# Self-attention's set-up reordered: coarse maxima first, sent by halves, and maxima 8 couples ahead instead of 10

## The chip, the cores and the metric

The kernel runs on one core of one Trainium2 chip. The metric is the device time of one execution in microseconds (us), median over several runs. All times below are microseconds from the span's start unless they say otherwise.

## The reference, cut to what matters

The whole reference is a decoder of two layers (self-attention, cross-attention and a feed-forward part in each, with layer norms between them). The change touches only the first self-attention:

```python
NUM_HEADS = 16                                   # x is (2, 1024, 256), heads of 16
q = x @ Wq.T * (1.0 / jnp.sqrt(D)); k = x @ Wk.T; v = x @ Wv.T
scores = jnp.einsum('bqhd,bkhd->bhqk', q, k)     # 1024 x 1024 for each of 2 x 16 heads
attn = jax.nn.softmax(scores, axis=-1)
out = jnp.einsum('bhqk,bkhd->bqhd', attn, v).reshape(B, S, D)
return out @ Wff.T + bff
x = _layernorm(x + _L0_attn_ref(x, ...), axis=-1)
```

## The kernel before, in words

The kernel is a row of stages, one after the other, and `stage_a` is the first self-attention. A generator, `schedule()`, yields jobs in one order, and each engine's function walks the whole list and does its own part of each job. So the order of the list is the order of work on PE (`tensor`), DVE (`vector`), ACT (`scalar`), POOL (`gpsimd`) and SP (`sync`), and an engine that waits holds back all that stands behind it in its own list.

**Jobs of the set-up.** `xt` i transposes one 128-row tile of X on PE, and ACT copies it to XT. `prep` (b, gi, half, which) is a projection of 512 columns: two matmuls in f32 (four instructions) for Q (`which` 0) or K (`which` 1). ACT writes the coarse part (a_QH or a_KH, fp32r), and DVE writes the rest (a_QL or a_KL, the result less the coarse part). `stack` k sends twelve pieces of 128 KB from these into QS[k % 3] and KS[k % 3]: for each of two head groups e, three blocks of 16 rows. Q holds coarse, fine, coarse, and K holds coarse, coarse, fine, so that one matmul over 48 rows gives a product of nearly full precision. For k = 0, SP sends six and ACT sends six; a later k goes by SP alone, for k of 2 and more as single `part` jobs spread over units. `edges` (DVE: 11 operations, then four transposes on PE) and `parts` (DVE: copies and small operations on their result) prepare a scatter into a matrix `adj` in DRAM, which a later stage reads; `prep_v` projects V.

**Jobs of the steady part.** There are 16 units u (batch, group of four heads, half of the queries). Unit u has 16 couples `s` (u, j): two matmuls of scores, and one DVE reduction over 128x1024 that gives row maxima (a_MX, line 741). `row` u folds them (a_MM), `m` u transposes the result, ACT copies it to a_MT, and SP sends it to DRAM (a_m), waits for that landing and sends it back as row 48 of QS, twice. Then come the unit's 16 slots n with two jobs `st` each: a matmul over 64 rows that gives the scores less the maximum, transposed, and ACT's exponential to a_P (line 847). `pv` multiplies by V. In slot n the schedule also yields a couple `s` of a unit ahead: ten couples ahead of `st` in the kernel before, with `row` u + 1 in slot 5 and `m` u + 1 in slot 8. `spread` (slot 3), `recip` (slot 7) and `scale` handle the softmax sums of unit u - 1 through DRAM (a_s, a_SQ, a_RQ, a_r, a_RB), on SP's queue as well. The `part` jobs stand in slots 4 to 15 of units 1, 2, 4, 6, 8 and 10, and a `prep` may overwrite the coarse and fine parts only after the pieces read from them have landed (`stacked`).

The list `between` puts jobs between the couples `s` that are done ahead of the first `st`. PE takes the banks 0 to 3 in pairs for `s` and `prep` of k = 0, and the banks 4 to 6 in turn for `st`, `xt`, `prep_v` and others.

Of the kernel before, what the change touches and what calls it, by code (L numbers as in the profile page):

```python
# [8 lines left out]
F32 = mybir.dt.float32  # L9
# [397 lines left out]
def stage_a(K, block):  # L407
# [33 lines left out]
    stack_in = [K.landing() for _ in range(3)]  # L441
    m_out = [K.landing() for _ in range(2)]
# [14 lines left out]
    U = [(b, g4, qh) for b in range(2) for g4 in range(4) for qh in range(2)]  # L457

    def schedule():
        for i in range(8):  # L460
            yield "xt", i
        for half in range(2):
            for which in range(2):
                yield "prep", 0, 0, half, which
        yield "powers",
        yield "stack", 0
        yield "edges",
        for kt in range(3):
            yield "prep_v", 0, kt
        yield "parts",  # L470
        between = {10: [("stack", 1)], 12: [("ctx", 0), ("ctx", 1)]}
        for kt in range(3, 8):
            between.setdefault(kt - 2, []).append(("prep_v", 0, kt))
# [4 lines left out]
        for i in range(6):  # L478
            between.setdefault(14 + 2 * i, []).append(("zero", i))
# [28 lines left out]
        for j in range(10):  # L508
            yield "s", 1, j
            yield from between.get(16 + j, ())  # L510
        for u in range(16):
            for n in range(16):
                yield "st", u, n, 0
                if n < 6 and u + 1 < 16:
                    yield "s", u + 1, n + 10
                if n >= 6 and u + 2 < 16:
                    yield "s", u + 2, n - 6
                if n == 5 and u + 1 < 16:
                    yield "row", u + 1
                yield "st", u, n, 1  # L520
                if n == 8 and u + 1 < 16:
                    yield "m", u + 1
                if n == 1 and u:
                    yield "pv", u - 1, 7
                    yield "turn_ou", u - 1
                if n > 1 and n % 2:
                    yield "pv", u, n // 2 - 1
                yield from late.get((u, n), ())
                if u:
                    if n == 3:  # L530
                        yield "spread", u - 1
                    if n == 7:
                        yield "recip", u - 1
                    if n == 11:
                        yield "scale", u - 1
                if n % 4 == 2 and step < E.LOTS:
                    yield "edge", step
                    step += 1
                if n % 8 == 0:
                    k = 2 * u + n // 8  # L540
                    yield "sums", k
                    if k % 8 == 7:
                        yield "lot", k // 8
                if n in (1, 6, 11):
                    yield "send", u, n
# [35 lines left out]
    def stacked(b, gi):  # L581

        k = 4 * b + 2 * gi
        return [(stack_in[i % 3], 12 * (i // 3 + 1)) for i in (k - 2, k - 1) if i >= 0]

    def tensor(_):
        free = {}

        def bank_free(bk):
            if bk in free:  # L590
                pe.wait_ge(*free[bk])

        for job in jobs:
# [44 lines left out]
            elif kind == "s":  # L638
# [5 lines left out]
                pe.wait_ge(stack_in[k % 3], 12 * (k // 3 + 1))  # L644
                bank_free(bk)
                for e in range(2):
                    rows = slice(64 * e, 64 * e + 48)
                    ins = mm(pe, bank(bk + e), QS[k % 3][rows, cc, qh * 512 + qt * 128:qh * 512 + qt * 128 + 128],
                             KS[k % 3][rows, cc, 512 * kh:512 * kh + 512])
# [8 lines left out]
            elif kind == "st":  # L658
# [4 lines left out]
                pe.wait_ge(m_in[u % 2], 2 * (u // 2 + 1))  # L663
                bank_free(bk)
# [43 lines left out]
    def vector(_):  # L708
        for i in range(2):
            v.e.memset(KS[i][:, :, :].bitcast(F32), 1.0)  # L710
            v.e.memset(QS[i][:, :, :].bitcast(F32), 0.0).then_inc(*fill[i].up())
# [7 lines left out]
        for job in jobs:  # L719
# [10 lines left out]
            elif kind == "edges":  # L730
# [65 lines left out]

    def scalar(_):
        s.wait_ge(eps_pool, 1)
        for job in jobs:
# [23 lines left out]
            elif kind == "powers":  # L823
                E.powers_act(s)
            elif kind == "stack" and a[0] == 0:
                for i in range(1, 12, 2):
                    stack(s, 0, i)
# [39 lines left out]
    def gpsimd(_):  # L867
# [6 lines left out]
        g.step(g.e.memset(KS[2][:, :, :].bitcast(F32), 1.0))  # L874
        g.step(g.e.memset(QS[2][:, :, :].bitcast(F32), 0.0), fill[2])
# [31 lines left out]
    def sync(_):  # L907
        def load_x(i):
            dma(sp, X[:, 4 * i:4 * i + 4, :],
                A["x"].rearrange("b (t p) d -> p (b t) d", p=128)[:, 4 * i:4 * i + 4, :]).then_inc(*x_in[i].up())  # L910

        def load(n, W, landed):
            dma(sp, W, A[n].rearrange("(c p) n -> p c n", p=128)).then_inc(*landed.up())

        load_x(0)
        load_x(1)
        load("L0_attn_WqT", WL[0], wq_in)
        load("L0_attn_WkT", WL[1], wk_in)
        load("L0_attn_WvT", WV[:, :, :], wv_in)
        load_x(2)  # L920
        load_x(3)
        E.edges_sp(sp)
        dma(sp, CX, A["ctx_1024"].rearrange("b s d -> s b d")).then_inc(*cx_in.up())
        for job in jobs:
            kind, *a = job
            if kind == "stack":
                for i in range(0, 12, 1 if a[0] else 2):
                    stack(sp, a[0], i)
            elif kind == "part":
                stack(sp, *a)  # L930
            elif kind == "weights":

                for k in (6, 7):
                    sp.wait_ge(stack_in[k % 3], 12 * (k // 3 + 1))
# [2654 lines left out]
```

## Time and profile before

| | |
|---|---|
| median of 3 runs | 2444.74 us (2443.32 to 2446.77) |
| span of the profiled execution | 2451.3 us (no other time is given with it) |
| PE, DVE, ACT, POOL busy | 93%, 62%, 45%, 43% of the span |
| first matmul | 4.92 us |
| first reduction of maxima | 34.44 us |
| first `st` of unit 0 | 70.08 us |
| first `st` of unit 15 | 473.16 us |

The profile is of one execution. It has a timeline for each engine, busy times by window with TensorE's granted clock (as a share of 2.4 GHz), waits by releaser, and the chain of work that ended last, which goes back from the last instruction to whatever released each step.

### The profile page before, as it was taken

To read this page: it belongs to the slowest core of one execution; us is meant where nothing else is said; L and a number is where in the kernel's file an instruction comes from. 1 tells how busy PE (TensorE), PEld (TensorE's weight loads), DVE (VectorE), ACT (ScalarE), POOL (GpSimd) and SP (SyncE) were. 2 spreads that over 40 slices of the span, in tenths; PEclk is the share of its full clock that TensorE was granted. 3 is DMA by queue.
4 is the path that set the end of the run, shared out by engine and by line. 5 is a ranking of instruction groups with operands and counts; after the bars stand their busy time and mean duration, and the time that the engine had idled before them with its cause. 6 is when DMAs were issued, how large, how long until landed. Compare 5 with 4: busy or idle time off the path is not lost.

```text
span 2451.3 us, 34108 instructions
## 1 busy us (share of the span) xinstructions
PE 2287.7 (93%) x12918; PEld 1434.3 (59%) x12918; DVE 1509.6 (62%) x2293; ACT 1106.9 (45%) x2365; POOL 1062.9 (43%) x780
## 2 busy tenths in 40 slices
PE   6999999989988999999999999999899789979998
PEld 3333343367754555554655555787666657768887
DVE  6778678457744666665666676722344566565556
ACT  1567657733322444443344444332321467643323
POOL 2446546624443788884578786333301122100000
PEclk8899999999999999999999999999899899989999
DMA  6454333232110011112010111254300601020001
GB/s 127 120 98 87 73 68 74 64 90 48 1 18 1 11 15 15 15 28 44 1 15 11 15 15 20 78 159 103 86 2 25 154 24 45 1 65 14 1 1 35
DMA packets 137613, 114.21 MB, mean 47 GB/s; under 512 B 74501, under 2 KB 114931, under 8 KB 137065
## 3 DMA queue, kind: packets, MB, share of 16 engines
q1 hardware_dynamic: 100297, 111.08, 16.7%
q0 software_dynamic: 36864, 0.15, 4.3%
q8 instruction: 103, 1.69, 0.3%
q10 hardware_dynamic: 288, 0.79, 0.2%
q14 instruction: 61, 0.50, 0.1%
HBM read 85.99 MB, written 13.39 MB: 41 GB/s over the span
## 4 chain that ended last, share of the span: by engine, by line
PE 73%; DMA 11%; DVE 8%; ACT 4%; issue 2%; SPq 2%; POOL 0%; ACTq 0%; DVEq 0%; POOLq 0%
PE PS L128 70%; DMA adj<-e_EE,e_IX 8%; SPq L154 2%; PE PS L1248 1%; DVE a_MX L741 1%; DVE c_MX L1896 1%; ACT a_P L847 1%; DVE g_SS L132 1%; DMA a_KS<-a_KL 1%; DMA a_r<-a_RQ 1%; PE PS L360 1%; DVE c_AC L132 1%; DVE g_st L1339 0%; ACT g_SS L1433 0%; PE PS L361 0%
## 5 line engine op out<-in xcount | busy, mean ns | idle before, releaser
L353 POOL DMA_INDIRECT adj<-e_EE,e_IX x256 | 416.9, 1629 | 400.8 <-DMA adj<-e_EE,e_IX 345.9
L1896 DVE TENSOR_REDUCE c_MX<-PS 128x2 f32<-128x1024 f32 x256 | 313.0, 1222 | 176.2 <-PE PS L128 176.2
L132 POOL TENSOR_TENSOR c_AC<-c_AC,c_P 128x1024 f32<-128x1024 f32 x145 | 364.3, 2513 | 77.6 <-DVE c_AC L132 70.5
L1993 ACT ACTIVATE c_P<-PS 128x1024 f32<-128x1024 f32 x256 | 252.0, 1026 | 214.8 <-PE PS L128 214.8
L741 DVE TENSOR_REDUCE a_MX<-PS 128x2 f32<-128x1024 f32 x256 | 303.2, 1219 | 55.3 <-PE PS L128 54.2
L847 ACT ACTIVATE a_P<-PS 128x512 f32<-128x512 f32 x512 | 270.6, 601 | 87.2 <-PE PS L128 86.4
L128 PE MATMUL PS<-c_P,c_VV 128*64 128x512 f32 x1024 | 247.7, 605 | 0.0
L137 POOL TENSOR_SCALAR e_EQ<-e_KR,e_KC 128x128 bf16<-128x128 f32 x256 | 162.8, 636 | 159.4 <-DMA e_KR<-adj_key 121.5
L128 PE MATMUL PS<-a_QS,a_KS 64*128 64x512 f32 x512 | 194.3, 461 | 20.9 <-ACT a_P L847 8.8
L128 PEld LDWEIGHTS PS<-a_QS,a_KS 64*128 64x128 f32 x512 | 84.1, 189 | 172.2 <-ACT a_P L847 96.8
L128 PE MATMUL PS<-a_KS,a_QS 48*128 48x512 f32 x512 | 171.3, 477 | 10.0 <-DMA a_QS<-a_QH 4.8
L128 PE MATMUL PS<-a_P,a_VA 128*32 128x512 f32 x1024 | 139.7, 618 | 0.0
L128 PE MATMUL PS<-c_KH,c_QH 64*128 64x512 f32 x512 | 119.6, 460 | 12.5 <-DVE c_MX L1896 12.5
L128 PEld LDWEIGHTS PS<-c_P,c_VV 128*64 128x64 f32 x1024 | 62.2, 136 | 116.1 <-issue 115.7
L128 PEld LDWEIGHTS PS<-c_KH,c_QH 64*128 64x128 f32 x512 | 48.3, 184 | 126.4 <-DVE c_MX L1896 62.4
L128 PE MATMUL PS<-h_XH,h_WH 128*128 128x512 f32 x256 | 101.4, 396 | 4.4 <-DVE h_XL L132 2.3
L128 PE MATMUL PS<-c_MR,c_ON 64*128 64x512 f32 x512 | 101.8, 390 | 2.3 <-DMA c_MR<-c_m 2.3
L128 PE MATMUL PS<-c_QH,c_KH 64*128 64x512 f32 x512 | 102.9, 397 | 0.0
L128 PE MATMUL PS<-c_QL,c_KH 64*128 64x512 f32 x512 | 101.9, 392 | 0.0
L128 PE MATMUL PS<-c_QH,c_KL 64*128 64x512 f32 x512 | 101.5, 390 | 0.0
L128 PE MATMUL PS<-h_XH,h_WL 128*128 128x512 f32 x256 | 100.9, 394 | 0.0
L128 PE MATMUL PS<-h_XL,h_WH 128*128 128x512 f32 x256 | 100.5, 393 | 0.0
(496 smaller groups left out, 4589.7 us busy)
## 6 DMA issues: line engine op xcount, KB each, us to landing
e_KR<-adj_key SPq DMA_DIRECT2D x64, 256.0 KB, 3.9
f_W<-in_L_ffn_w SPq DMA_DIRECT2D x16, 1024.0 KB, 7.5
c_RB<-c_r SPq DMA_DIRECT2D x58, 128.0 KB, 2.8
g_FB<-in_fside_1x16xSxS SPq DMA_DIRECT2D x8, 616.0 KB, 8.6
a_QS<-a_QH SPq DMA_DIRECT2D x32, 128.0 KB, 3.9
adj<-e_zt SPq DMA_DIRECT2D x16, 256.0 KB, 4.2
adj<-e_EE,e_IX POOLq DMA_INDIRECT x256, 3.2
d_AJ<-adj SPq DMA_DIRECT2D x8, 512.0 KB, 9.0
```

Source lines behind the costliest of these rows:

```text
L128: return pe.e.matmul(o, l, r, start=first, stop=last, skip_group_check=True)
L132: return v.e.tensor_tensor(o, a, b, op)
L137: return v.e.tensor_scalar(o, a, s1, None, op0)
L154: return q.e.dma_start(raw(o), raw(i))
L353: g.e.indirect_dma_start(self.adj, bass.IndirectOffsetOnAxis(ap=self.IXE[:, k:k + 1], axis=0), self.EE[:, k:k + 1], None, compute_op=ALU.a ...
L360: pe.e.transpose(K.bank(bk)[:, 0:128], src[:, k, 0:128], K.ident[:, :])
L741: v.e.reduce_max(MX[:, u % 2, :, cc, qt, kh], bank(bk, 2).rearrange("p (e n) -> p e n", e=2), AX, negate=True).then_inc(*smax_dve.up())
L847: s.e.activation(PB[t % NP][:, e, :], bank(bk), ACT.Exp, scale=1.0 / 16).then_inc(*st_act.up())
L1248: ins = pe.e.transpose(bank(bk)[0:n, 128 * j:128 * j + 128], flat[:, 512 * q + 128 * j:512 * q + 128 * j + n], K.ident[:, :])
L1896: v.e.reduce_max(MX[:, w % 2, :, qt, kh], bank(0, 2).rearrange("p (h n) -> p h n", h=2), AX, negate=True).then_inc(*smax_dve.up())
L1993: s.e.activation(PB[t % NP][:, :, :].rearrange("p h n -> p (h n)"), bank(2 + 2 * (t % 2), 2), ACT.Exp, scale=0.125).then_inc(*st_act.up())
```

## The change

It does five things. (1) SP's loads are in another order: the weights of Q and K ahead of the second part of x, and the edges ahead of V's weights. DVE clears only KS[0] and QS[0]; POOL clears those of k = 1 as well. (2) The set-up does the first half (four `xt`, `prep` Q and K of half 0), then a new job `high` 0, then the edges' jobs, then the second half (K ahead of Q) and `high` 1. `high` sends only the coarse parts of one half into rows 0 to 15 of each head group: two pieces of 64 KB by SP (Q) and two by ACT (K). It waits for ACT's coarse parts, not for DVE's. (3) `stack` 0 sends the remaining eight pieces (`LOWER`), four on each queue. (4) The couples `s` of the first two units (k = 0) work on 16 rows, the coarse parts alone, and wait only for the halves that they read. The maxima serve as the shift of the exponent, and `st` still works on all rows; it waits for all pieces. (5) Couples run 8 ahead of `st`, not 10: 24 instead of 26 stand ahead of the first `st`; `row` moves from slot 5 to 7 and `m` from slot 8 to 10. All eight `prep_v` now stand between the couples (three stood ahead of them).

```diff
+    AHEAD = 8
     def schedule():
-        for i in range(8):
+        for i in range(4):
             yield "xt", i
-        for half in range(2):
-            for which in range(2):
-                yield "prep", 0, 0, half, which
         yield "powers",
+        yield "keys",
+        for which in range(2):
+            yield "prep", 0, 0, 0, which
+        yield "high", 0
+        yield "edges",
+        yield "parts",
+        for i in range(4, 8):
+            yield "xt", i
+        for which in (1, 0):
+            yield "prep", 0, 0, 1, which
+        yield "high", 1
         yield "stack", 0
-        yield "edges",
-        for kt in range(3):
-            yield "prep_v", 0, kt
-        yield "parts",
-        for kt in range(3, 8):
-            between.setdefault(kt - 2, []).append(("prep_v", 0, kt))
+        for kt in range(8):
+            between.setdefault(kt, []).append(("prep_v", 0, kt))
...
-        for j in range(10):
+        for j in range(AHEAD):
             yield "s", 1, j
...
-                if n < 6 and u + 1 < 16:
-                    yield "s", u + 1, n + 10
-                if n >= 6 and u + 2 < 16:
-                    yield "s", u + 2, n - 6
-                if n == 5 and u + 1 < 16:
+                if n < 16 - AHEAD and u + 1 < 16:
+                    yield "s", u + 1, n + AHEAD
+                if n >= 16 - AHEAD and u + 2 < 16:
+                    yield "s", u + 2, n - (16 - AHEAD)
+                if n == 15 - AHEAD and u + 1 < 16:
                     yield "row", u + 1
-                if n == 8 and u + 1 < 16:
+                if n == 18 - AHEAD and u + 1 < 16:
                     yield "m", u + 1
...
-                pe.wait_ge(stack_in[k % 3], 12 * (k // 3 + 1))
+                if k:
+                    pe.wait_ge(stack_in[k % 3], stacks(k))
+                else:
+                    for half in sorted({qh, kh}):
+                        pe.wait_ge(high_in[half], 4)
...
-                    rows = slice(64 * e, 64 * e + 48)
+                    rows = slice(64 * e, 64 * e + (48 if k else 16))
...
-        for i in range(2):
-            v.e.memset(KS[i][:, :, :].bitcast(F32), 1.0)
-            v.e.memset(QS[i][:, :, :].bitcast(F32), 0.0).then_inc(*fill[i].up())
+        v.e.memset(KS[0][:, :, :].bitcast(F32), 1.0)
+        v.e.memset(QS[0][:, :, :].bitcast(F32), 0.0).then_inc(*fill[0].up())
...
+    def high(q, half, which):
+        q.wait_ge(prep_act, 2 * half + 2)
+        q.wait_ge(fill[0], 1)
+        cols = slice(512 * half, 512 * half + 512)
+        for e in range(2):
+            dma(q, (QS, KS)[which][0][64 * e:64 * e + 16, :, cols], HL[2 * which][32 * e:32 * e + 32, cols]).then_inc(
+                *high_in[half].up())
+    LOWER = [i for i in range(12) if i // 2 % 3]
...
         load_x(0)
-        load_x(1)
         load("L0_attn_WqT", WL[0], wq_in)
         load("L0_attn_WkT", WL[1], wk_in)
+        load_x(1)
+        E.edges_sp(sp)
         load("L0_attn_WvT", WV[:, :, :], wv_in)
         load_x(2)
         load_x(3)
-        E.edges_sp(sp)
```

## Rows read from the trace of the kernel before

**Rows 1.** The page: the chain that ended last, by engine and by line
```profile
PE 73%; DMA 11%; DVE 8%; ACT 4%; issue 2%; SPq 2%; POOL 0%; ACTq 0%; DVEq 0%; POOLq 0%
PE PS L128 70%; DMA adj<-e_EE,e_IX 8%; SPq L154 2%; PE PS L1248 1%; DVE a_MX L741 1%; DVE c_MX L1896 1%; ACT a_P L847 1%; DVE g_SS L132 1%; DMA a_KS<-a_KL 1%; DMA a_r<-a_RQ 1%; PE PS L360 1%; DVE c_AC L132 1%; DVE g_st L1339 0%; ACT g_SS L1433 0%; PE PS L361 0%
```
**Rows 2.** The chain in order of time, 5 to 72: start, us, what
```profile
25.83 7.84 DMA a_QS<-a_QH
```
**Rows 3.** Timeline of the set-up: start, us, engine, instruction, idle before and releaser
```profile
6.96 0.92 ACT L808 COPY XT<-PS 128x256 f32<-128x256 f32 x3
9.35 0.52 DVE L715 COPY a_WQ<-a_P 128x256 f32<-128x256 f32 x2
9.92 3.74 PE L128 MATMUL PS<-XT,a_WQ 128*128 128x512 f32 x4
13.49 1.88 PE L128 MATMUL PS<-XT,a_WK 128*128 128x512 f32 x4
20.07 0.28 DVE L214 CAST e_EH<-e_ER 128x256 f32<-128x256 int32 x1
22.19 2.33 ACTq L154 DMA_DIRECT2D a_KS<-a_KH  x2
25.37 0.42 DVE L230 COPY e_KC<-PS 128x256 f32<-128x256 f32 x1 [1.21 <-PE PS L251]
29.71 0.16 DVE L142 SCALAR_TENSOR_TENSOR e_TH<-e_GP,e_PL 128x1 f32<-128x1 f32 x1
```
**Rows 4.** Timeline of DVE's maxima ahead of unit 0, and PE's first `st`
```profile
34.44 2.36 DVE L741 TENSOR_REDUCE a_MX<-PS 128x2 f32<-128x1024 f32 x2 [4.57 <-PE PS L128]
42.97 1.23 DVE L741 TENSOR_REDUCE a_MX<-PS 128x2 f32<-128x1024 f32 x1 [1.50 <-PE PS L128]
45.10 1.23 DVE L741 TENSOR_REDUCE a_MX<-PS 128x2 f32<-128x1024 f32 x1 [0.91 <-PE PS L128]
46.60 8.02 DVE L741 TENSOR_REDUCE a_MX<-PS 128x2 f32<-128x1024 f32 x7 [0.27 <-PE PS L128]
58.62 0.18 DVE L146 TENSOR_REDUCE a_MM<-a_MX 128x16 f32<-128x32 f32 x1
70.08 0.63 PE L128 MATMUL PS<-a_QS,a_KS 64*128 64x512 f32 x1
```
**Rows 5.** Windows (PE alone): us, PE busy, granted clock, DMA share, GB/s
```profile
4.00:10.00 6.00, 3.98 (x17) 1.00 1.10 364
33.70:44.20 10.50, 10.49 (x25) 0.51 0.89 144
```
**Rows 6.** Windows of units 13 and 15: us, PE, PEld, DVE, ACT, POOL busy
```profile
428.98:451.12 22.14, 21.56 (x149) 8.53 (x145) 19.37 (x19) 17.53 (x37) 16.42 (x21) 1.00 0.27 66
473.13:494.30 21.17, 17.56 (x112) 5.75 (x112) 2.05 (x8) 16.66 (x35) 6.57 (x5) 1.00 0.39 113
```
**Rows 7.** The chain in order of time, 74 to 260: transfers until they landed
```profile
139.03 4.05 DMA a_r<-a_RQ
154.52 5.69 DMA a_KS<-a_KL
195.29 2.69 DMA a_r<-a_RQ
```
**Rows 8.** Timeline of PE at the starts of units 3 and 5
```profile
149.22 0.50 PE L128 MATMUL PS<-a_QS,a_KS 64*128 64x512 f32 x1 [0.64 <-DMA a_QS<-a_m]
205.74 0.50 PE L128 MATMUL PS<-a_QS,a_KS 64*128 64x512 f32 x1
```
**Rows 9.** Timeline of SP: the maxima's way back, and one piece
```profile
146.54 1.25 SPq L154 DMA_DIRECT2D a_QS<-a_m  x2
147.83 0.62 SPq L154 DMA_DIRECT2D a_QS<-a_QH  x1
201.66 1.25 SPq L154 DMA_DIRECT2D a_QS<-a_m  x2
```
**Rows 10.** Timeline of ACT in unit 3, slot 4
```profile
160.32 0.59 ACT L816 CAST a_QH<-PS 128x512 fp32r<-128x512 f32 x1 [3.68 <-DMA a_KS<-a_KL]
```

More of the change, by code:

```diff
@@ L441, in stage_a @@
     stack_in = [K.landing() for _ in range(3)]
+    high_in = [K.landing() for _ in range(2)]
     m_out = [K.landing() for _ in range(2)]
@@ L478, in schedule @@
         for i in range(6):
-            between.setdefault(14 + 2 * i, []).append(("zero", i))
+            between.setdefault(13 + 2 * i, []).append(("zero", i))
         late = {(15, 12): [("weights",)], (0, 0): [("wf",)]}
@@ L583, in stacked, with stacks @@
         k = 4 * b + 2 * gi
-        return [(stack_in[i % 3], 12 * (i // 3 + 1)) for i in (k - 2, k - 1) if i >= 0]
+        return [(stack_in[i % 3], stacks(i)) for i in (k - 2, k - 1) if i >= 0]
+    def stacks(k):
+        return 12 * (k // 3 + 1) - (0 if k % 3 else 4)
     def tensor(_):
@@ L663, in tensor @@
                 pe.wait_ge(m_in[u % 2], 2 * (u // 2 + 1))
+                if k == 0:
+                    pe.wait_ge(stack_in[0], stacks(0))
+                    pe.wait_ge(high_in[1], 4)
                 bank_free(bk)
@@ L729, in vector @@
                 tt(v, L[:, cols], bank(bk), H[:, cols].bitcast(F32), ALU.subtract).then_inc(*prep_dve.up())
-            elif kind == "edges":
+            elif kind == "keys":
                 E.setup_dve(v)
@@ L824, in scalar @@
                 E.powers_act(s)
+            elif kind == "high":
+                high(s, a[0], 1)
             elif kind == "stack" and a[0] == 0:
-                for i in range(1, 12, 2):
+                for i in LOWER[1::2]:
                     stack(s, 0, i)
@@ L873, in gpsimd @@
         g.step(g.e.memset(VA[:, :, :, :], 1.0), va_pool)
-        g.step(g.e.memset(KS[2][:, :, :].bitcast(F32), 1.0))
-        g.step(g.e.memset(QS[2][:, :, :].bitcast(F32), 0.0), fill[2])
+        for i in (1, 2):
+            g.step(g.e.memset(KS[i][:, :, :].bitcast(F32), 1.0))
+            g.step(g.e.memset(QS[i][:, :, :].bitcast(F32), 0.0), fill[i])
         g.step(g.e.memset(K.onesf[:, :], 1.0), ones_pool)
@@ L926, in sync @@
             if kind == "stack":
-                for i in range(0, 12, 1 if a[0] else 2):
+                for i in range(12) if a[0] else LOWER[0::2]:
                     stack(sp, a[0], i)
+            elif kind == "high":
+                high(sp, a[0], 0)
             elif kind == "part":
@@ L933, in sync @@
                 for k in (6, 7):
-                    sp.wait_ge(stack_in[k % 3], 12 * (k // 3 + 1))
+                    sp.wait_ge(stack_in[k % 3], stacks(k))
                 K.W0.load(sp, A, "k", "L0_xattn_Wk")
```

## The prediction

> **What bounds the kernel now.** First the page's chain: PE and DMA carry 73% and 11% of it, and 8% is the scatter into adj, in a later stage [rows 1]. The stages follow each other and the scatter's calls have fixed places in POOL's list, so time that the first attention saves or loses should move all that follows by as much. I therefore need only this stage.
>
> Then the chain and the timeline of its start. PE's projections end near 19 (13.49 and three more spans of about 1.8) [rows 3]; then the twelve pieces are issued and land, and the last 7.84 us of that are one wait, to 33.67 [rows 2]. The first maxima reduction starts at 34.44, the row of maxima of unit 0 is folded at 58.62, and `st` starts at 70.08 [rows 4]. Between these DVE's reductions set the pace where it is dense (8.02 us for 7, so 1.15 each), and PE sets it where a `prep_v` stands between: a couple and a `prep_v` took 1.23 + 1.50 = 2.73 us while the clock was 1.2 GHz (0.51 granted up to 44.2), and 1.50 us (45.10 to 46.60) at 2.4 GHz [rows 4, 5].
>
> Last, the steady part. Unit 13 took 22.14 us, and unit 15, which has no couples left, 21.17 [rows 6]. So the couples cost about 1 us in 16 slots: the exponentials and their matmuls set that pace.
>
> **The change, step by step, ahead of the first `st`.**
>
> Start. DVE now clears two tiles before it copies the weights, so the copies no longer wait till 9.35 [rows 3]. At the 364 GB/s of the loads [rows 5], weights that stand ahead of the second x (512 KB) come 1.4 us sooner. ACT bounds it next: its first copies run from 6.96, three in 0.92 us, so four are done by about 8.4 [rows 3]. Q's projection starts there instead of 9.92. It took 3.74 us at 1.2 GHz, and K's 1.88 at 2.4 GHz [rows 3]; with a mix for K I put its coarse part at 15.0. `high` 0 is issued at 15.1 and I let 4.5 us pass until it has landed: 19.6 (the shortest chain for small transfers took 2.69 us [rows 7], pieces of 128 KB in a queue 5.69 [rows 7]). The half itself needs only coarse parts, so DVE's subtraction is off this path.
>
> DVE's edge work moves between: 11 operations, 20.07 to 24.16 (the 1.21 us idle ahead of 25.37), so 4.1 us; then 25.37 to 29.87, 4.5 us [rows 3]. The first fits beside PE's projections. The second now runs from about 15.8 to 20.3, ahead of DVE's two subtractions of half 1. PE does four transposes and four `xt` from 15.1 on (ACT first issues two pieces), then K and Q of half 1, 1.88 us each [rows 3]: 18.0 to 21.7. Q's coarse part is at 22.2, its fine part at 22.9, and the first reduction can start at 22.9 instead of 34.44: 11.5 us sooner. `high` 1 lands by about 27; couple 8, the first to need it, comes some 12 us after 22.9, so it is hidden.
>
> Couples 0 to 15. Before: 34.44 to 58.62 = 24.2 us with five `prep_v` between. Now eight stand there. PE has been dense since 18, so I take 2.4 GHz: 8 x 1.50 = 12.0 us. ACT has six pieces to issue first (two took 2.33 us [rows 3], so about 5.5 in all, to 28), and its first V copy is late by about 1 us for the fourth bank. Then 8 x 1.20 = 9.6. Together 22.6, and row 0 is at 45.5: 13.1 us sooner. At 1.2 GHz throughout, the eight cost 8 x 2.73 = 21.8 and row 0 is at 55.3.
>
> From row 0 to `st` was 11.46 us with ten couples; eight leave 11.46 - 2 x 1.15 = 9.2. So `st` at 54.7, **15.4 us sooner**. The last two couples of the kernel are not lost work: they move into slots that had none, at (22.14 - 21.17)/16 = 0.06 us each [rows 6].
>
> The Trainium skill (DMA: Bandwidth & Descriptors, Anatomy of one DMA) gives a transfer about 2.0 us of fixed cost plus its bytes at 436 GB/s, which speaks against halves: the fixed cost comes twice. By an estimate from that page a 64 KB piece takes 2.15 us, and `high` 0 would land 2.5 us sooner than I have it; by the same rule the second fixed cost lies in `high` 1, which is hidden. The sum stays, since DVE at 22.9 and not the landing is the last to come.
>
> **The steady part.** Row and `m` move two slots back: 2 x 22.14/16 = 2.8 us. In SP's list `recip` u - 1 (slot 7) stands ahead of `m`, with a round trip: slot 8 of unit 2 lies eight slots of 1.38 us ahead of 149.22, at 138.2, and a_r landed only at 139.03 + 4.05 = 143.08 [rows 7, 8]. SP came late there, not PE, and in units without pieces I take the 2.8 us as hidden behind that. In units 1, 2, 4 and 6 two more pieces now stand ahead of `m` on SP: 2 x 0.62 us of issue [rows 9], and a_m's small transfer goes right behind them. What that costs a small transfer: a_r took 4.05 us right behind pieces and 2.69 where there was a gap [rows 7], so 1.4 more. Together 2.6 us late.
>
> Unit 5: its maxima were sent by 202.91 and `st` began at 205.74; in unit 3, which waited for them, `st` came 1.43 after the sending's end (149.22 less 147.79) [rows 8, 9]. So unit 5 had 205.74 - 202.91 - 1.43 = 1.4 us to spare, and loses 1.2. Unit 2 is similar with some 2 us to spare and loses 0.6. Units 3 and 7 have none to spare, but there a `prep` waits for pieces anyway: ACT sat idle 3.68 us for the landing of the last one [rows 7, 10]. A late start eats that wait, and only the 1.4 us by which SP's wait for a_m now holds the remaining pieces is left, twice. Sum 1.2 + 0.6 + 2.8 = 4.6. For it, `s` of unit 4 needs its pieces two slots later, which gives back about 0.5. Net **4.1 us lost**; its bounds are 0 (the queue is empty enough) and 2.6 at each of four units plus as much again, about 10.
>
> **Sum.** 15.4 - 4.1 = 11.3 us. The sum is made on an execution whose span is 2451.3 us, 6.6 above the median of the runs; the stage's durations are taken as the same there. 2444.74 - 11.3 = 2433.4, say 2433.
>
> **Rivals.**
> The maxima are not late. If a_m is sent as before in spite of the pieces, the whole 15.4 us and the 0.5 come through: 2429. For it: the wait for maxima at unit 3 is only 0.64 us now [rows 8]. Against it: SP's queue has no gap ahead of `m` in those units. 20%.
>
> The clock takes it back. PE was busy 10.49 of 10.50 us from 33.7 and still had 0.51 granted [rows 5]. If it has that over the eight `prep_v`, 9.8 us of 11.3 are gone: 2443. For it: PE is idle in parts between 15 and 18, while DVE and ACT work. Against it: before the stretch at 33.7 PE had been idle for nearly 5 us (DVE's 4.57 us behind it) [rows 4], and here it is not. 13%. The Trainium skill (TensorE: Matmul & The Clock Gate, Part 1) says that the default state is throttled and activity releases it. By that rule the dense work from 18 on would get the full clock, as in the sum; the rows show that it can take 10 us.
>
> It ends slower: the lead of eight is too short everywhere. If `recip`'s round trip moves back with `row` (both are in slot 7 now, on one DVE), then SP comes to `m` 2.8 us later in all units. Where 1.4 us are to spare, each of some eleven units of ordinary length loses 1.4; that alone takes back 15.4. It ends slower once the delay passes 2.8 us, that is with another 0.5 us in each; at 3.5 us it costs 11 x 2.1 = 23, so 2452. Against it: DVE is busy 19.37 of 22.14 us [rows 6], so it has room, and the row is a 0.18 us operation [rows 4]. 5%.
>
> Nothing comes of the reorder: the first couples start early, but the remaining pieces or the maxima of unit 0 land late behind 24 pieces, and `st` waits. The pieces ahead of unit 0 and 1 need about as much transfer time as before and start at 22; `st` would be held only if they landed after 55. The twelve of unit 0 took from 20.2 to 33.67 [rows 2], so 24 take some 27 us, to 49. 4%, 2444.
>
> **Chances.** The forecast's case 55%, maxima not late 20%, clock 13%, slower 5%, nothing 4%, other 3%. A measurement of this kernel tells about 0.2% (4.9 us) from no change. Faster by more: 0.55 + 0.20 + some of the clock's case and the rest, 0.84. Within: 0.11. Slower: 0.05. Range: from 2427 (all comes through and K's projection runs warm, 2 us more) to 2441 (bound of 10 us in the steady part, or most of the clock's price).
>
> **What would show it.** The first reduction near 23; periods of 1.5 us over the first eight; a_MM near 45.5; `st` near 55. A `st` that waits for a_QS<-a_m at units 2, 3, 5 and 7 and nowhere else. The last `st` of unit 15 some 11 us sooner, and every later stage as long as before. I am wrong if the clock stays at 1.2 GHz over the `prep_v`, if SP is behind at `m` in all units, or if the gain at `st` of unit 0 is not there at the end.

## The result, and the profile after

The kernel after took 2463.33 us (median of 11 runs, 2448.04 to 2471.91), the kernel before 2446.31 (11 runs, 2441.83 to 2453.92). The ratio is 1.0057, with a 95% interval of 1.0035 to 1.0079. I had forecast 2433 and faster; it is slower by about 14 us on the mean (the medians lie 17 us apart), and its runs lie further apart than those of before.

The profiled execution of after has a span of 2462.3 us, 11.0 more than before's 2451.3. Where they stand against each other, read from the start of the first `st` of a unit:

| | before | after | difference | forecast |
|---|---|---|---|---|
| first reduction of maxima | 34.44 | 25.11 | -9.3 | -11.5 |
| row 0 folded | 58.62 | 53.95 | -4.7 | -13.1 |
| `st` of unit 0 | 70.08 | 63.42 | -6.7 | -15.4 |
| `st` of unit 1 | 103.72 | 107.44 | +3.7 | -15.4 |
| `st` of unit 15 | 473.16 | 481.75 | +8.6 | -11.3 |
| span | 2451.3 | 2462.3 | +11.0 | -11.3 |

So the gain ahead of unit 0 is real but less than half of what I had summed, unit 0 turns it into a loss, and units 1 to 14 add 4.9 us to that. What is there at unit 15 is also there at the end, to 2.4 us.

The timeline of the start of after (DVE, POOL and PE), to be held against [rows 3]:

```profile
5.67 1.80 POOL L904 MEMSET a_KS<- 128x2048 f32 x1
5.78 3.74 DVE L731 COPY a_WQ<-a_P 128x256 f32<-128x256 f32 x2 [0.62 <-DMA a_P<-in_L_attn_WqT]
9.42 1.83 POOL L904 MEMSET a_KS<- 128x2048 f32 x1
9.43 3.85 DVE L731 COPY a_WK<-a_P 128x256 f32<-128x256 f32 x2
9.57 3.78 PE L128 MATMUL PS<-XT,a_WQ 128*128 128x512 f32 x4 [1.27 <-DVE a_WQ L731]
13.34 2.09 PE L128 MATMUL PS<-XT,a_WK 128*128 128x512 f32 x4
17.36 0.42 DVE L142 SCALAR_TENSOR_TENSOR e_EL<-e_EL,e_EH 128x256 f32<-128x256 f32 x1
17.84 0.44 PE L249 MATMUL PS<-ident,e_EL 128*128 128x128 f32 x2 [2.40 <-DVE e_EL L142]
```

The weights were there at 5.78, as planned. But each of four copies, which took 0.3 us before, now takes 1.9: one for each POOL memset that runs beside it. DVE's first part of the edge work ends at 17.8, and PE waits 2.40 us for it: the transposes of that part stand ahead of the second half's `xt` in PE's list. The sum had them start at 15.1.

Then DVE, ACT and PE over the V projections, to be held against [rows 4]:

```profile
25.11 2.39 DVE L757 TENSOR_REDUCE a_MX<-PS 128x2 f32<-128x1024 f32 x2
27.76 1.23 DVE L757 TENSOR_REDUCE a_MX<-PS 128x2 f32<-128x1024 f32 x1 [0.26 <-PE PS L128]
28.23 1.69 ACTq L154 DMA_DIRECT2D a_KS<-a_KL  x1
29.25 1.23 DVE L757 TENSOR_REDUCE a_MX<-PS 128x2 f32<-128x1024 f32 x1 [0.26 <-PE PS L128]
30.01 0.92 ACT L863 COPY a_VA<-PS 128x256 f32<-128x256 f32 x3 [5.54 <-issue]
30.43 1.88 PE L128 MATMUL PS<-a_WV,XT 128*128 128x256 f32 x4 [1.22 <-ACT a_VA L863]
35.81 1.23 DVE L757 TENSOR_REDUCE a_MX<-PS 128x2 f32<-128x1024 f32 x1 [1.50 <-PE PS L128]
38.54 1.23 DVE L757 TENSOR_REDUCE a_MX<-PS 128x2 f32<-128x1024 f32 x1 [1.50 <-PE PS L128]
53.95 0.18 DVE L146 TENSOR_REDUCE a_MM<-a_MX 128x16 f32<-128x32 f32 x1
```

The period starts at 1.49 us (27.76 to 29.25), ACT is held by the issue of its six pieces till 30.01, PE waits 1.22 us for it, and from then on the period is 2.73. The windows of after (PE alone) show what changed: the granted clock.

```profile
13.60:30.60 17.00, 12.39 (x45) 1.00 0.51 99
30.70:42.00 11.30, 11.30 (x26) 0.50 1.04 133
63.40:85.20 21.80, 21.80 (x57) 0.50 0.32 104
85.30:107.40 22.10, 20.45 (x99) 0.92 0.20 68
```

TensorE had 2.4 GHz from 13.6 to 30.7, and 1.2 GHz from 30.7 to 85.3, although the profile has it busy for every bit of the last 21.8 us. Before, the full clock was back about 8 us after the first `st`.

Last, the maxima: the wait lines of PE's weight loads for a_QS<-a_m had 3.8 us in three times before and have 13.5 in five now. The timeline of PE and SP at unit 2 of after, against [rows 8, 9]:

```profile
126.39 0.59 SPq L154 DMA_DIRECT2D a_KS<-a_KL  x1
127.03 0.58 SPq L154 DMA_DIRECT2D a_m<-a_MT  x1
129.99 1.24 SPq L154 DMA_DIRECT2D a_QS<-a_m  x2
132.61 0.50 PE L128 MATMUL PS<-a_QS,a_KS 64*128 64x512 f32 x1 [2.69 <-DMA a_QS<-a_m]
```

### The profile page after: what moved, and what is told of

It is laid out like the page before. It is cut to its first block, busy times and chain, and to the rows that moved or that the text cites. A ratio compares the mean times of both kernels' runs of the same rounds, so it can differ in the third digit from the quotient of the medians.

```text
span 2462.3 us, 34114 instructions
## 1 busy us (share of the span) xinstructions
PE 2299.6 (93%) x12918; PEld 1434.8 (58%) x12918; DVE 1513.3 (61%) x2291; ACT 1108.2 (45%) x2365; POOL 1068.2 (43%) x782
## 4 chain that ended last, share of the span: by engine, by line
PE 74%; DMA 10%; DVE 8%; ACT 4%; issue 2%; SPq 1%; POOL 0%; ACTq 0%; DVEq 0%; POOLq 0%
PE PS L128 71%; DMA adj<-e_EE,e_IX 8%; PE PS L1280 1%; ACT a_P L876 1%; DVE c_MX L1928 1%; SPq L154 1%; DVE g_SS L132 1%; DVE a_MX L757 1%; PE PS L360 1%; DVE c_AC L132 1%; DMA a_r<-a_RQ 1%; DMA a_m<-a_MT 0%; DVE g_st L1371 0%; ACT g_SS L1465 0%; PE PS L361 0%
## 5 line engine op out<-in xcount | busy, mean ns | idle before, releaser
L128 PE MATMUL PS<-a_QS,a_KS 64*128 64x512 f32 x512 | 203.9, 475 | 25.9 <-ACT a_P L876 12.0
L128 PE MATMUL PS<-a_KS,a_QS 48*128 48x512 f32 (+1 forms) x512 | 176.0, 486 | 1.9 <-DVE a_MX L757 1.3
```

Of the source, the lines that this page charges most:

```text
L128: return pe.e.matmul(o, l, r, start=first, stop=last, skip_group_check=True)
```

## The experiments

Each of the twelve kernels was timed against the kernel before on the same chip. Chips differ: before had medians from 2446 to 2455, so only ratios are compared. All start from after or before as named. First the readings of all of them, then each.

| run | rows in unit 1's couples | lead | `st` of unit 0 | full clock back after it | unit 0 | units 1 to 14 | ratio (95% interval) |
|---|---|---|---|---|---|---|---|
| before | 48 | 10 | 70.08 | 8.3 | 33.6 | 369.4 | 1 |
| after | 16 | 8 | 63.42 | 21.9 | 44.0 | 374.3 | 1.0057 (1.0035 to 1.0079) |
| after, lead 10 | 16 | 10 | 61.22 | 22.3 | 42.1 | 368.2 | 0.9992 (0.9975 to 1.0009) |
| after, POOL late | 16 | 8 | 64.12 | 21.1 | 42.1 | 381.9 | 1.0040 (1.0019 to 1.0061) |
| after, 48 rows | 48 | 8 | 62.99 | 7.8 | 33.3 | 381.8 | 1.0013 (1.0003 to 1.0023) |
| before, lead 8 | 48 | 8 | 65.86 | 7.4 | 33.2 | 378.7 | 1.0038 (1.0026 to 1.0050) |
| 48 rows, lead 10 | 48 | 10 | 61.42 | 7.4 | 33.3 | 369.0 | 0.9977 (0.9955 to 0.9998) |
| 48 rows, pieces behind | 48 | 8 | 66.51 | 7.6 | 33.3 | 372.9 | 0.9985 (0.9966 to 1.0003) |
| 48 rows, lead 10, POOL last | 48 | 10 | 61.79 | 8.4 | 33.7 | 369.6 | 0.9959 (0.9942 to 0.9977) |
| the same, pieces by SP ("best") | 48 | 10 | 54.77 | 8.5 | 33.8 | 370.8 | 0.9943 (0.9920 to 0.9965) |
| before, 16 rows | 16 | 10 | 72.78 | 9.4 | 36.4 | 368.5 | 1.0026 (1.0007 to 1.0044) |
| best, lead 8, pieces behind | 48 | 8 | 53.13 | 7.8 | 33.3 | 378.4 | 0.9958 (0.9942 to 0.9974) |
| best, 16 rows | 16 | 10 | 55.54 | 9.1 | 36.2 | 371.4 | 0.9978 (0.9963 to 0.9993) |
| best, 32 rows | 32 | 10 | 54.90 | 22.1 | 42.0 | 369.9 | 0.9962 (0.9947 to 0.9977) |

Columns but the last are of one profiled execution each, in us; "units 1 to 14" is from unit 1's first `st` to unit 15's. From unit 15's first `st` to the end, thirteen of the fourteen profiles take 1974 to 1982 us; the exception is named below.

**Lead 10 in the kernel after.**

```diff
-    AHEAD = 8
+    AHEAD = 10
```

> The kernel after, with AHEAD back at 10 and all else kept. Theory (the shorter lead makes the maxima late): the waits of PE for a_QS<-a_m at the starts of units 2, 3, 5 and 7 (13.5 us in total for the weight load in the profile after) fall to about the 3.8 us of before, st of unit 0 begins 2.3 us later, and the time falls by 5 to 9 us, to about 2456. Rival (the loss is the clock in unit 0 alone): unit 0 stays at about 44 us, the waits for maxima cost nothing, and the time stays at 2463 or rises by 2. Second rival (the late maxima are the whole loss): the time falls to 2446 or below.

Measured: 0.9992, which is 0.65% (16 us) under the kernel after, more than the 5 to 9 us expected. By the time alone it is what the second rival gave (the late maxima are the whole loss). PE's weight loads wait 3.1 us for a_QS<-a_m, and units 1 to 14 are back at 368.2. But unit 0 still takes 42.1, so a second loss is left, which the earlier start (61.22) makes up for. In time the lead is worth more than the 6.1 us that the two profiles show in units 1 to 14. One more thing in this profile matters below, DVE and PE over the V projections:

```profile
32.82 1.13 PE L128 MATMUL PS<-a_WV,XT 128*128 128x256 f32 x4 [1.61 <-ACT a_VA L863]
37.41 1.23 DVE L757 TENSOR_REDUCE a_MX<-PS 128x2 f32<-128x1024 f32 x1 [0.26 <-PE PS L128]
38.90 1.23 DVE L757 TENSOR_REDUCE a_MX<-PS 128x2 f32<-128x1024 f32 x1 [0.27 <-PE PS L128]
```

PE waits 1.61 us for ACT where it waited 1.22 in the kernel after, and yet the clock stays at 2.4 GHz (25.4 to 45.9) and the period at 1.49. This execution had its 1.2 GHz earlier, from 18.6 to 25.4, with the same order of work up to there; its first reduction is at 27.58. So the place of the low clock in the set-up differs between executions.

**POOL's clearing behind DVE's copies.**

```diff
+        g.wait_ge(wp_dve, 2)
         for i in (1, 2):
             g.step(g.e.memset(KS[i][:, :, :].bitcast(F32), 1.0))
```

> The kernel after, with POOL's clearing of KS and QS for k = 1 and 2 held back until DVE has copied both weights; nothing else changes. Theory (DVE's copies waited for POOL's memsets: 3.74 and 3.85 us for two copies each, where before they took 0.52 and 0.56): copies of about 0.5 us again, K's projection of half 0 directly behind Q's, and the first reduction of maxima 2 to 4 us sooner than 25.11, so 21 to 23. Rival (the copies are slow because transfers land in the same memory at that time): they stay at 3.7 us. For the whole time I expect 2 to 4 us less if the clock falls at the same place, but the clock's fall at 30.67 may move, which is worth more than that either way.

The copies are short again, and the block has moved. The timeline of DVE and POOL in this run:

```profile
5.62 0.49 DVE L731 COPY a_WQ<-a_P 128x256 f32<-128x256 f32 x2 [0.46 <-DMA a_P<-in_L_attn_WqT]
8.86 1.80 POOL L906 MEMSET a_QS<- 128x2048 f32 x1
9.19 1.62 DVE L214 CAST e_EH<-e_ER 128x256 f32<-128x256 int32 x1 [0.37 <-DMA e_EV<-in_L_attn_adj_vals]
10.72 1.83 POOL L905 MEMSET a_KS<- 128x2048 f32 x1
10.84 1.85 DVE L137 TENSOR_SCALAR e_EL<-e_EH 128x256 f32<-128x256 f32 x1
12.73 0.43 DVE L132 TENSOR_TENSOR e_EV<-e_EV,e_EL 128x256 f32<-128x256 f32 x1
```

The rival is out: transfers land at this time as before, and the copies take 0.25 each. DVE operations of one input, a cast and a TENSOR_SCALAR, now end with the memset beside them (10.81 and 12.69 where the memsets end at 10.66 and 12.55), while a TENSOR_TENSOR of two inputs takes its usual 0.43 at 12.73, beside the next memset (12.60 to 14.43). The first reduction stays at 25.64, not the 21 to 23 that I expected. In time, 1.0040 against 1.0057, the intervals overlap: this run alone settles nothing on the price.

**Unit 1's couples on 48 rows.**

```diff
                     for half in sorted({qh, kh}):
                         pe.wait_ge(high_in[half], 4)
+                    if u:
+                        pe.wait_ge(stack_in[0], stacks(0))
...
-                    rows = slice(64 * e, 64 * e + (48 if k else 16))
+                    rows = slice(64 * e, 64 * e + (48 if u else 16))
```

> The kernel after, with the couples of unit 1 on 48 rows as before (they also wait for the remaining pieces of k = 0); unit 0 stays on 16 rows. Theory (a couple over 16 rows counts as less activity, and so the granted clock of TensorE stays at 1.2 GHz from 30.67 to 85.28, where before it came back at 78.33, 8 us after the first st): the clock comes back sooner, within 10 us of the first st, and unit 0 takes about 34 us instead of 44; the time falls by 5 to 10 us. Rival (rows do not matter, the low clock lasts because of how the waits fall): clock low as long as in the kernel after, unit 0 near 44 us, time unchanged near 2463.

Unit 0 takes 33.3 instead of 44.0 and the clock is back 7.8 us after its first `st`. The time is 1.0013, 0.44% less. Its profiled execution took 381.8 in units 1 to 14, more than the 374.3 of after, and another 11 us more than before behind unit 15. It was the slowest of its eleven runs (2469.4 us, median 2456.8). By that one profile the edit would lose; all runs together say otherwise, with intervals that do not meet, and they decide.

**The kernel before with lead 8.** The six `zero` jobs move one place up in `between` as well; the change does the same, which its description leaves out.

```diff
-            between.setdefault(14 + 2 * i, []).append(("zero", i))
+            between.setdefault(13 + 2 * i, []).append(("zero", i))
...
-        for j in range(10):
+        for j in range(8):
...
-                if n < 6 and u + 1 < 16:
-                    yield "s", u + 1, n + 10
-                if n >= 6 and u + 2 < 16:
-                    yield "s", u + 2, n - 6
-                if n == 5 and u + 1 < 16:
+                if n < 8 and u + 1 < 16:
+                    yield "s", u + 1, n + 8
+                if n >= 8 and u + 2 < 16:
+                    yield "s", u + 2, n - 8
+                if n == 7 and u + 1 < 16:
...
-                if n == 8 and u + 1 < 16:
+                if n == 10 and u + 1 < 16:
                     yield "m", u + 1
```

> The kernel before, with couples 8 ahead instead of 10 (row in slot 7, m in slot 10) and its own set-up. Theory (the lead alone costs 5 to 10 us in the steady part and gains 2.3 in the set-up): 2449 to 2454, PE's waits for a_QS<-a_m over 10 us. Rival (the lead costs nothing by itself and the waits for maxima come from the other set-up): 2444, waits for a_QS<-a_m under 5 us.

Measured 1.0038 and 16.1 us of waits for a_QS<-a_m: the shorter lead costs 0.38% (9 us) in the old set-up, though `st` of unit 0 comes 4.2 us sooner. Units 1 to 14 take 9.3 us more. The rival is out. Where no wait is left, a unit is longer too, as the windows of unit 13 in the kernel after show against unit 13 in [rows 6]:

```profile
436.95:459.34 22.39, 21.77 (x149) 8.57 (x145) 19.23 (x19) 17.60 (x36) 16.06 (x21) 1.00 0.24 61
```

22.39 against 22.14: from slot 8 to 11, before took 1.67 + 1.66 + 0.58 + 2.03 = 5.94 us and after 1.18 + 1.91 + 1.18 + 1.91 = 6.18 from `st` to `st`. `m` shared slot 8 with the `sums` before; now it disturbs a slot of its own.

**Both edits.** AHEAD = 10 and 48 rows in unit 1.

> The kernel after with both single edits at once: couples 10 ahead and unit 1's couples on 48 rows. Theory (the two losses are separate: late maxima in the steady part, low clock in unit 0): st of unit 0 begins near 61, unit 0 takes 33 to 35 us, units 1 to 7 as in the kernel before, and the time is 7 to 11 us below the kernel before, ratio 0.995 to 0.997. Rival (the low clock in unit 0 does not depend on the rows, and the run on 48 rows was a lucky one): unit 0 takes 42 us as with the lead alone, ratio 0.999.

0.9977, unit 0 at 33.3, units 1 to 14 at 369.0. In the profile both losses go. The gain is a little short of the 0.995 to 0.997 that I expected: together the two edits bring 0.80%, while alone they bring 0.65% and 0.44%. The four intervals, 0.1% to 0.2% to either side, cover that difference. This profile too has 2.4 GHz over the V projections (24.5 to 41.6) in spite of a wait of 1.67 us for ACT.

**Two pieces less ahead of the maxima**, on the 48-row version with lead 8.

```diff
-                at(max(2 * k - 4, 1), 4 + i, "part", k, i)
+                at(max(2 * k - 4, 1), (4 if i < 4 else 6) + i, "part", k, i)
```

> The kernel after with unit 1's couples on 48 rows (as in the run of that edit alone) and lead 8; the part jobs from the fifth on stand two slots later, so that again only four pieces stand ahead of m on SP, and six again behind it in slots 10 to 17. Theory (it is the two pieces directly ahead of the maxima's small transfers that make them late): PE's waits for a_QS<-a_m fall from 17.2 us to 5 or less, the starts of units 2, 3, 5, 6 and 7 follow the unit before without a gap, and the time falls by 5 to 8 us against that run. Rival (m itself, two slots later, is too late, whatever stands ahead of it): the waits stay above 10 us and the time within 2 us.

The waits fall from 17.2 us to 5.5, and the ratio from 1.0013 to 0.9985 (the intervals, 1.0003 to 1.0023 and 0.9966 to 1.0003, just touch). The timeline of SP and PE at unit 2, first the 48-row version with the pieces ahead, then this one:

```profile
116.42 0.59 SPq L154 DMA_DIRECT2D a_KS<-a_KL  x1
117.05 0.58 SPq L154 DMA_DIRECT2D a_m<-a_MT  x1
120.02 1.24 SPq L154 DMA_DIRECT2D a_QS<-a_m  x2
122.54 0.79 PE L128 MATMUL PS<-a_QS,a_KS 64*128 64x512 f32 x1 [3.76 <-DMA a_QS<-a_m]
```

```profile
118.63 0.42 SPq L154 DMA_DIRECT2D a_m<-a_MT  x1
120.51 1.25 SPq L154 DMA_DIRECT2D a_QS<-a_m  x2
123.22 0.49 PE L128 MATMUL PS<-a_QS,a_KS 64*128 64x512 f32 x1 [0.98 <-DMA a_QS<-a_m]
```

Behind a piece, a_m holds SP for 2.97 us; without one, for 1.88. PE's idle time goes from 3.76 to 0.98.

**POOL's clearing last**, on the version with 48 rows and lead 10, the pieces in their old places.

```diff
+        g.wait_ge(E.vp_dve, 1)
         for i in (1, 2):
             g.step(g.e.memset(KS[i][:, :, :].bitcast(F32), 1.0))
```

> The kernel with lead 10 and 48 rows in unit 1, and POOL's clearing of k = 1 and 2 held back until DVE's last operation for the edges (vp) is done, so that no memset runs beside DVE's copies or edge operations. Theory (a DVE operation of one input from the buffers of fp32 waits for a POOL memset that is running): copies 0.5 us for two, edge operations 0.3 each (none of 1.4 to 1.8), the edges' first part ends near 13.5 instead of 17.8, and the first couple is at 20 to 22 instead of 24.2. Rival (the first couple is set by the projections and ACT alone): 24. For the time: 1 to 4 us less than with lead 10 and 48 rows alone, if the clock stays.

The timeline of DVE and POOL:

```profile
6.32 0.50 DVE L733 COPY a_WK<-a_P 128x256 f32<-128x256 f32 x2 [0.21 <-DMA a_P<-in_L_attn_WkT]
9.47 0.29 DVE L214 CAST e_EH<-e_ER 128x256 f32<-128x256 int32 x1 [2.33 <-DMA e_EV<-in_L_attn_adj_vals]
13.14 0.43 DVE L142 SCALAR_TENSOR_TENSOR e_EL<-e_EL,e_EH 128x256 f32<-128x256 f32 x1
19.55 1.80 POOL L907 MEMSET a_KS<- 128x2048 f32 x1 [13.94 <-DVE e_VP L240]
```

No DVE operation is stretched, the first edge part ends at 13.57 as I had put it, and the first reduction is at 22.43 (I had forecast 22.9 for the kernel after). The profiles fall into two groups by this: the kernel after and the five versions of it with memsets in this stretch have the first reduction at 24.6 to 28.2 (24.6 and 25.1 where the clock stayed at 2.4 GHz up to there), and the five with POOL last have it at 22.4 to 23.1. 0.9959 against 0.9977: the direction is as expected, the intervals overlap.

**All remaining pieces of k = 0 by SP**, on top of that.

```diff
-                for i in LOWER[1::2]:
-                    stack(s, 0, i)
+                pass
...
-                for i in range(12) if a[0] else LOWER[0::2]:
+                for i in range(12) if a[0] else LOWER:
```

> As the run before this one, and all eight remaining pieces of k = 0 go by SP, so that ACT issues only the four of the coarse parts. Theory (ACT was held up to 30.01 by its queue's pieces, PE waited 1.2 us for the first V copy, and the clock fell at 30.67): PE does not wait there, the clock stays at 2.4 GHz over most of the eight V projections, with periods of 1.5 instead of 2.73 us, and row 0 comes 3 to 6 us sooner. Rival (the clock falls with sparse couples anyway, the wait is chance): clock falls at about the same place, row 0 at most 1 us sooner.

The timeline of ACT and DVE:

```profile
21.84 1.49 ACTq L154 DMA_DIRECT2D a_KS<-a_KH  x2
23.43 0.37 ACT L864 COPY a_VA<-PS 128x256 f32<-128x256 f32 x1 [1.62 <-PE PS L128]
30.59 1.23 DVE L759 TENSOR_REDUCE a_MX<-PS 128x2 f32<-128x1024 f32 x1 [0.27 <-PE PS L128]
32.07 1.23 DVE L759 TENSOR_REDUCE a_MX<-PS 128x2 f32<-128x1024 f32 x1 [0.26 <-PE PS L128]
43.31 0.19 DVE L146 TENSOR_REDUCE a_MM<-a_MX 128x16 f32<-128x32 f32 x1
```

The period is 1.48 us over all V projections, the clock falls at 36.0 when they are done, and row 0 is at 43.3 instead of 50.3 in the run before. All four profiles with the pieces by SP keep 2.4 GHz to 36.0 or later. Of the seven in which ACT issues them, five lose it within 1.5 us of PE's wait for ACT and two do not (lead 10, and 48 rows with lead 10). This is the fastest version by its median: 2435.51 us, ratio 0.9943 (0.9920 to 0.9965), 14 us below the kernel before. It is not clear of the run before, 0.9959 (0.9942 to 0.9977).

**16 rows in the kernel before.**

```diff
-                    rows = slice(64 * e, 64 * e + 48)
+                    rows = slice(64 * e, 64 * e + (16 if u == 1 else 48))
```

> The kernel before with one edit: the couples of unit 1 multiply over 16 rows instead of 48, with every wait, transfer and place as before. Theory (a matmul over fewer rows counts as less activity, so the clock comes back late): st of unit 0 begins at 70 as before, the granted clock stays at 1.2 GHz until unit 1's last couples are done near 84 or beyond instead of 78.33, unit 0 takes 40 us or more instead of 33.64, and the time rises by 6 to 10 us, ratio 1.003. Rival (rows do not matter; it was the order of the set-up): clock back at 78, unit 0 at 33.6, ratio 1.000.

One number in the kernel before makes it slower by 0.26%. But the profile does not fit my theory of it: the clock came back 9.4 us after the first `st`, hardly later, and unit 0 took 36.4, not 40. `st` of unit 0 also came 2.7 us later, which the edit should not touch.

**Lead 8 on the best version**, with the pieces from the fifth on two slots later, as above.

> The best version so far (48 rows in unit 1, POOL's clearing behind the edges' operations, all remaining pieces of k = 0 by SP) with lead 8 instead of 10 and the part jobs from the fifth on two slots later. Theory (a lead of 8 gains 2.3 us ahead of unit 0 and loses 0.24 us in each unit, since m then has slot 10 for itself instead of sharing slot 8 with the sums, and a few us more in waits for a_m): 2 to 6 us slower than with lead 10, ratio 0.995 to 0.997. Rival (with the pieces out of the way the shorter lead pays): 1 to 3 us faster, ratio 0.993.

0.9958, in the middle of what the theory gave; the waits for a_QS<-a_m are 2.1 us in total. Its interval overlaps with that of the best version (0.9943), but in the profiles units 1 to 14 take 7.6 us more. No gain of the shorter lead is shown even with the pieces out of its way.

**16 and 32 rows in the best version.**

> The best version (lead 10, 48 rows in unit 1, POOL's clearing last, pieces by SP) with unit 1's couples back on 16 rows; their waits stay. Theory (fewer rows, later return of the clock): the clock, which came back at 63.31 with 48 rows, comes back at 70 or later, unit 0 takes 38 to 44 us instead of 33.8, and the time rises by 5 to 10 us, ratio 0.997 to 0.998. Rival (rows do not matter here): unit 0 at 33.8 and ratio 0.994.

> The same with 32 rows in unit 1's couples. Theory (it goes by the rows): between the 48-row version (unit 0 33.8 us, ratio 0.9943) and the 16-row version. Rival (only a matmul over very few rows matters, or none): as one of the two.

0.9978 and 0.9962 against 0.9943. 16 rows are slower than 48 by the median, as in the kernel before; here the intervals overlap by 0.0002. The time is what my theory gave and the profile is not: with 16 rows the clock came back at 64.6 and not at 70 or later. 32 lies between by its median, but its profile has unit 0 at 42.0, and its interval overlaps with both. So rows do not act by their count. What they do stands in the timeline of PE, slot 0 of unit 0, both at 1.2 GHz; first 48 rows, then 16:

```profile
54.77 0.62 PE L128 MATMUL PS<-a_QS,a_KS 64*128 64x512 f32 x1
55.31 0.79 PE L128 MATMUL PS<-a_KS,a_QS 48*128 48x512 f32 x2
55.91 0.62 PE L128 MATMUL PS<-a_QS,a_KS 64*128 64x512 f32 x1
56.46 0.38 PE L128 MATMUL PS<-e_VP,e_EQ 128*128 128x5 bf16 x8
```

```profile
55.54 0.79 PE L128 MATMUL PS<-a_QS,a_KS 64*128 64x512 f32 x1
56.26 0.80 PE L128 MATMUL PS<-a_KS,a_QS 16*128 16x512 f32 x2
56.98 0.79 PE L128 MATMUL PS<-a_QS,a_KS 64*128 64x512 f32 x1
57.71 0.38 PE L128 MATMUL PS<-e_VP,e_EQ 128*128 128x5 bf16 x8
```

From `st` to couple to `st` to the next instruction takes 0.54, 0.60 and 0.55 us with 48 rows and 0.72, 0.72 and 0.73 with 16, so 0.48 us more in the slot; the couple itself takes 0.79 or 0.80 with either. All profiles agree on this slot: six with 16 or 32 rows take 2.48 us for it, and eight with 48 take 1.85 to 2.00. At 2.4 GHz the difference is there too: slot 4 takes 0.85 us with 16 rows and 0.57 with 48 in these two versions. I read it as lost overlap: with 48 rows a matmul can begin while its neighbour still runs.

## Why the prediction was wrong, step by step

**Right.** The loads' new order (weights at 5.78), the early coarse transfers (never waited for), the shape of the gain from two couples less (row 0 to `st` 9.47 us, forecast 9.2), and that a change at the stage's end carries through the later stages. `high` by halves is in the fastest version too; no run tests it alone.

**DVE's copies and edge work (forecast: the copies no longer wait, edge work 4.1 us beside the projections).** I costed the move of two memsets to POOL at nothing, since POOL was free. The runs with POOL held back show that they stretch DVE's operations of one input, 1.9 us for 0.3. It came to the path over PE's 2.40 us wait for the edge work. In this profile it is 2.2 us of the missing 8.7 ahead of unit 0: 25.11 against 22.9, and 22.43 with POOL last. The Trainium skill (SBUF — State Buffer, SBUF: two separate sides) says so: VectorE and GpSimd share a port pair under an exclusive lock held for the whole instruction, which concerns DVE operations in a two-port mode, and those of two inputs only against a GpSimd operation that reads. The traces agree on both halves: copies, a cast and a TENSOR_SCALAR are held to the memset's end, and a TENSOR_TENSOR takes 0.43 us beside a memset, which reads nothing. I should have drawn on it for this step.

**Eight projections of V at 1.50 us.** I named the clock as a rival at this place (13%) and took the wrong side for five of the eight: 2.73 against 1.50, or 6.2 us, which with the 2.2 and 0.3 more gives the 8.7. I had seen that ACT must issue six pieces first, and priced it as 1 us; it was 1.22 us of idle PE, and the clock fell right behind it. With ACT free the clock held to the last projection, in four profiles of four. But a wait of PE for ACT does not by itself make the clock fall: two profiles kept 2.4 GHz through waits of 1.61 and 1.67 us, both of which had been at 1.2 GHz for 6.8 us some 6 us ahead of the wait; a third (48 rows, pieces behind) had been as well and lost it at 33.1. What decides where the clock falls stays open.

**Unit 0 (forecast: as before).** The largest miss, 10.4 us in the profile. The sum goes from `st` of unit 0 straight to the steady part and so puts what 16 rows do among the 64-row matmuls of `st` at nothing, without a reason. No rival covered it. Fourteen profiles divide without exception: eight with 48 rows in unit 1's couples have unit 0 at 33.2 to 33.8 us, six with 16 or 32 have 36.2 to 44.0 (before and after counted in). The edit alone is worth 0.26% in the kernel before and 0.44% taken out of the kernel after, both clear of noise, and 0.35% in the best version, just not clear.

Two parts can be told apart. The longer slots are shown above at either clock: the 16-row profiles where the clock came back within 9.4 us have unit 0 at 36.2 and 36.4, some 2.6 us over 33.7. The rest, up to 44, is there when the clock comes back only after 21 to 22 us. In all fourteen it comes back during a projection of four f32 matmuls over 128 rows or up to 0.6 us behind it: the unit's first in ten profiles, its second, some 13 us later, in the other four. Why it is the second in four of these six and in none of the eight stays open; my theory that few rows count as little activity is not borne out, since the two profiles with an early return have 16 rows and one with a late return has 32.

The Trainium skill (TensorEngine Tiling (Array Packing), Available Configurations and Key Properties) has a rule that fits the first part: the array works in modes of 128, 64 or 32 rows, and changing the mode drains it. If `st` and 48 rows are in the mode of 64 and 16 and 32 rows are not, the traces agree: 16 and 32 rows give the same 2.48 us in slot 0, 0.48 us over 48 rows for three steps at 1.2 GHz. That the rows of a matmul set its mode is read from this. The rule does not give all of it: the third step, from `st` to a matmul over 128 rows, leaves the mode of 64 in both versions and is 0.18 us longer as well.

**The maxima (forecast: 2.6 us late, 4.1 us in all).** The mechanism was right, at the units that I named (2, 3, 5 and 7). In the profile of after the size is near too, 4.9 us in units 1 to 14. But unit 10 came 3.4 us shorter there than before, for which I have no reason, and between the other versions the lead costs more than that (7.6 and 9.3 us in units 1 to 14). The issue of two pieces and 1.1 to 1.3 us more for a_m is what I had summed. The piece run confirms it (17.2 to 5.5 us). What I left out is that SP came later still to `m`. In unit 1 of the lead-8 version of before, `recip`'s last transfers (a_RB) were issued 3.3 us later within the unit, and with the two pieces and a_m the maxima of unit 2 were sent 5.9 us later than before, where I had 2.6.

Then, 0.24 us in a unit without waits since `m` lies alone in slot 10, at most some 3 us in all, which I had not seen. And behind each of the four long waits (2.6 to 3.6 us of the weight loads) the clock was low: in the kernel after it is at 1.2 GHz from 133.1 to 139.9 and from 160.4 to 167.2, right behind the starts of units 2 and 3. The lead is worth 0.38% in the kernel before (9 us) and 0.65% out of the kernel after (16 us), for 4.1 forecast less the 2.3 that two couples less gain ahead of unit 0. The absorption that I counted on in units 3 and 7 is there (34.3 to 32.7 us and 35.4 to 31.7).

**The transfers of `high` 0.** The fit that I took from the Trainium skill (DMA: Bandwidth & Descriptors, Anatomy of one DMA) stands there for transfers issued by GpSimd, and these go by SP and ACT. In the kernel after the first piece of 64 KB took 2.7 us to land and all four 3.9, between that estimate (2.15, so 2.35 us sooner and not the 2.5 that I wrote) and my 4.5. It was off the path either way.

**The sign.** The rival that ends slower had a part of it: in unit 1 of the kernel after, a_RB was issued 2.5 us later within the unit, as it feared. But it asked for that in every unit, and in unit 13 the maxima were sent only 0.4 us later and nothing waited. From the forecast's -11.3 to the profile's +11.0 it is 22.3 us: 8.7 ahead of unit 0, 10.4 in unit 0, 0.8 in units 1 to 14 and 2.4 behind them. The step that failed is therefore unit 0 on 16 rows first, then the V projections at 2.4 GHz and the memsets at no cost. By the times of the runs, the lead and the 16 rows are each enough to take the kernel after from slower to within 0.13% of before.

What stays open: why the clock falls early and comes back late in some executions, and with that why the kernel after scatters over 24 us where before scatters over 12.

## What to carry to other kernels

Here a matmul did not get cheaper with 16 contraction rows for 48, and the row of matmuls around it got dearer: look at what its neighbours on PE are, and keep interleaved matmuls in the same class of rows. A job moved to an idle engine is not free if, as POOL's memsets did, it holds up operations of an engine on the critical path, and a shorter lead must be checked against what then stands directly ahead of its small transfers in the queue. A reorder that gains early can be held against each of its parts alone: here the lead of 8 was worth 16 us out of the kernel after (1.0057 to 0.9992) and the 16 rows in unit 1 11 us (1.0057 to 1.0013), and with those two out, POOL's clearing last and ACT free of the pieces, the same set-up is 14 us faster than the kernel before.

## What the runs showed of the hardware

TensorE can stay at 1.2 GHz for 54.6 us (30.7 to 85.3), the last 21.9 of them with PE busy all the time by the profile. The Trainium skill (TensorE: Matmul & The Clock Gate, Part 1) says that activity releases the throttle; the trace shows a stretch where being busy by the profile was not enough. Versions that differ little got it back 7.4 or 22.3 us after the first `st`. A POOL memset of 128x2048 (1.8 us) stretches a DVE copy or TENSOR_SCALAR in fp32 from 0.3 to 1.9 us at most, to the memset's end, and leaves TENSOR_TENSOR at 0.43. Six issues of 128 KB or less from ACT's queue kept ACT from computing for 5.5 us while SP's queue was also sending.
